# Attention by rows of 512 queries, with pieces of the projections and of the output between the units

## What is computed

```
xn = ln(x, g_norm)
q = (xn @ Wq).reshape(b, n, HEADS, DIM_HEAD).transpose(0, 2, 1, 3)
k, v = split(xn @ Wkv)                      # one head of 64 each
k, v = concat([null_k, k]), concat([null_v, v])
q, k = l2norm(q) * q_scale, l2norm(k) * k_scale
sim = einsum('bhid,bjd->bhij', q, k) * 8 + rel_pos_bias        # causal
out = einsum('bhij,bjd->bhid', softmax(sim), v)
z = ln(merge_heads(out) @ Wout, g_out)
s = 127 / max(abs(z), axis=-1)
return x + (clip(round(z * s), -128, 127) / s) @ ternary.T * weight_scale + bias
```

## Time and profile before

| | us |
|---|---|
| median of 3 runs | 1786.13 (1785.21 to 1788.83) |
| the profiled execution | 1786.81 |
| its span, first to last instruction | 1784.5 |
| PE busy | 1604.5 |
| DVE busy | 1407.2 |
| ACT busy | 1141.8 |
| POOL busy | 1421.9 |

### The profile page before, as it was taken

One profiled execution on the slowest core, in us unless ns is written; L12 is line 12 of the kernel. 1 busy time (PEld: TensorE's weight loads), 2 busy tenths in 40 slices (PEclk: granted clock), 3 DMA queues, 4 the chain that ended last, 5 costly groups with the idle time before them and its releaser, 6 DMA issues.

```text
span 1784.5 us, 46777 instructions
## 1 busy us (share of the span) xinstructions
PE 1604.5 (90%) x15122; PEld 1079.6 (60%) x15122; DVE 1407.2 (79%) x2569; ACT 1141.8 (64%) x2195; POOL 1421.9 (80%) x934
## 2 busy tenths in 40 slices
PE   3786897899999999998995898799999999998997
PEld 1443554577777777776552455477777777776553
DVE  4885898788888888884765798688888888887576
ACT  1342555587787788777441555477887887787441
POOL 3564666799999999997673566799999999999574
PEclk9998999899999999998997999899999999999998
DMA  6000012011112111100023002021111111110023
GB/s 186 1 0 21 25 29 59 13 37 35 28 37 49 25 37 37 29 21 14 30 71 102 25 29 65 1 47 26 38 37 25 37 37 41 26 32 13 7 71 100
DMA packets 41302, 68.84 MB, mean 39 GB/s; under 512 B 8880, under 2 KB 9392, under 8 KB 41136
## 3 DMA queue, kind: packets, MB, share of 16 engines
q1 hardware_dynamic: 36512, 58.12, 13.3%
q10 hardware_dynamic: 4640, 8.54, 1.4%
HBM read 58.11 MB, written 8.54 MB: 37 GB/s over the span
## 4 chain that ended last, share of the span: by engine, by line
PE 44%; issue 26%; POOL 17%; DVE 9%; ACT 1%; DVEq 1%; POOLq 1%; DMA 1%; SPq 0%; ACTq 0%
PE ps L1162 21%; PE ps L1135 10%; PE ps L1138 10%; DVE work L930 5%; POOL rinv L491 4%; POOL work L496 4%; POOL work L523 3%; POOL qo L454 2%; POOL work L541 2%; PE ps L1204 1%; DVE work L958 1%; POOL rstd L486 1%; DVE denom L955 1%; POOL work L498 1%; POOL work L462 1%
## 5 line engine op out<-in xcount | busy, mean ns | idle before, releaser
L511 POOL TENSOR_TENSOR work<-work 128x1024 f16<-128x1024 f32 (+2 forms) x576 | 978.2, 1733 | 44.2 <-ACT work L644 41.6
L930 DVE SCALAR_TENSOR_TENSOR work<-ps,tab 128x1024 f32<-128x1024 f32 (+3 forms) x640 | 668.7, 1059 | 141.3 <-PE ps L1138 139.4
L644 ACT ACTIVATE work<-work 128x1024 f32<-128x1024 f32 (+3 forms) x640 | 578.2, 924 | 207.3 <-DVE work L930 203.4
L1162 PEld LDWEIGHTS ps<-vals,work 128*128 128x128 bf16 (+1 forms) x8704 | 545.3, 98 | 115.8 <-POOL work L511 2.2
L1162 PE MATMUL ps<-vals,work 128*128 128x129 f16 x8704 | 600.5, 221 | 1.9 <-POOL work L511 1.8
L1135 PE MATMUL ps<-qo,kT 128*128 128x512 f16 (+3 forms) x1280 | 344.2, 351 | 20.8 <-DVE work L930 15.0
L1138 PE MATMUL ps<-qo,kT 128*128 128x512 f16 (+3 forms) x1280 | 342.1, 349 | 0.0
L1106 PE MATMUL ps<-wq,work 128*128 128x512 f16 x768 | 178.0, 390 | 20.4 <-DVE work L863 20.4
L1138 PEld LDWEIGHTS ps<-qo,kT 128*128 128x128 f16 x1280 | 123.2, 98 | 117.5 <-issue 3.3
L1204 PE MATMUL ps<-wout,work 128*128 128x512 f16 x768 | 175.0, 385 | 0.0
L1106 PEld LDWEIGHTS ps<-wq,work 128*128 128x128 f16 x768 | 74.6, 100 | 113.5 <-issue 34.2
(11 more groups left out here) (131 smaller groups left out, 1727.0 us busy)
## 6 DMA issues: line engine op xcount, KB each, us to landing
tab<-bias_table SPq DMA_DIRECT2D x64, 512.0 KB, 4.7
work<-in_x SPq DMA_DIRECT2D x32, 256.0 KB, 2.6
tab<-in_x SPq DMA_DIRECT2D x32, 256.0 KB, 2.7
out_x<-work ACTq DMA_DIRECT2D x32, 256.0 KB, 2.2
work<-in_L_cond_Wq SPq DMA_DIRECT2D x1, 2048.0 KB, 12.8
work<-in_L_cond_Wout SPq DMA_DIRECT2D x2, 1024.0 KB, 10.3
qo<-in_L_cond_w SPq DMA_DIRECT2D x1, 1024.0 KB, 9.5
qo<-in_L_cond_b SPq DMA_DIRECT2D x2, 256.0 KB, 4.2
```

The costliest lines, as they stand in the source:

```text
L511: pool.tensor_tensor(low[:, k % LRING, :, c0:512], probs[:, r, :, c0:512], high[:, r, :, c0:512], ALU.subtract).then_inc(low_pool, 1)
L644: act.activation(probs[:, k % RING, :, c0:512], probs[:, k % RING, :, c0:512], ACT.Exp).then_inc(expd, 1)
L930: dve.scalar_tensor_tensor(out=probs[:, k % RING, :, c0:512], in0=ps[:, 2 * (k % 2):2 * (k % 2) + 2, c0:512], scalar=SCORE, in1=tab[:, :, ...
L1162: last = pe.matmul(ps[:, sum_bank(i, q), (t % SUMS) * VS:(t % SUMS + 1) * VS], parts[:, rings[part], e, s * P:(s + 1) * P], vals[:, j, :], ...
```

## The change

The loop over batches is gone, and the program is written out. The attention is one sequence of 640 units over eight rows of 512 queries (four of each batch), row by row: in a row the eight head pairs, in a head pair the units. Row 0 and row 4 (i = 0) have 32 units, rows 1 and 5 64, rows 2 and 6 96, rows 3 and 7 128. Before the first unit only the first 8 of the 32 projection tiles are done, as before, with a bank of its own for each step. The steps of the other 24 tiles, and of the first 28 of 32 output tiles, are given to slots, one slot for each unit. Two tables (`B_FROM`, `C_FROM`) say near which slot a tile starts, `B_STAGES` and `C_STAGES` in which order its steps come and with which gaps, and `spread` fills the slots: on PE at most one piece a slot, between `score` and `weigh`; on VectorE and ScalarE behind the slot's bias or exponential (ACT1: ahead of the exponential). All these pieces use one PSUM bank (7), and a piece waits until the one before it has been read out of the bank. Their working tiles are single. The last four output tiles follow the attention with banks of their own.

Also changed: the rings of `probs` and `low` have 8 and 6 places in place of 10 and 8, weighing follows 5 units behind; VectorE takes two low halves of a head pair in a row with i = 3, one with i = 2, none else; the transposed output is split into halves behind the transposition (out of PSUM, on ScalarE and VectorE); z is copied out of PSUM first, the gain is applied on VectorE, 1 / standard deviation goes into the scale of the quantisation; the bias table is loaded in pieces by a list. 308 pieces on PE wait for bank 7.

```diff
-TW = S
-NEARER = (0, 1, 5, 9)
...
+KS = 22
+ROWS = B * NB
+UNITS = [(r, hp, j) for r in range(ROWS) for hp in range(HP) for j in range(4 * (r % NB) + 4)]
 NU = len(UNITS)
-RING = 10
-LRING = 8
-WORK = 16912
-LAG = 6
+NUMBER = {u: n for n, u in enumerate(UNITS)}
+ROW_START = [NUMBER[r, 0, 0] for r in range(ROWS)] + [NU]
+RING = 8
+LRING = 6
+LAG = 5
...
+DVE_LOW = {3: (5, 11), 2: (5,), 1: (), 0: ()}
...
+WEIGH, DRAINS, NULLS, STORES = ({} for _ in range(4))
+for _n, (_r, _hp, _j) in enumerate(UNITS):
+    for _q in range(3):
+        WEIGH.setdefault(_n + LAG + late(_q, _j), []).append((_n, _q))
+for _r in range(ROWS):
+    for _hp in range(HP):
+        _end = NUMBER[_r, _hp, 4 * (_r % NB) + 3]
+        for _q in range(3):
+            DRAINS.setdefault(_end - 2 + _q + LAG + 1, []).append((_r, _hp, _q))
+        NULLS[_end - 2] = (_r, _hp)
+        STORES[_end + LAG + 2] = (_r, _hp)
+LAST_SLOT = NU + LAG + 3
+AHEAD = 8
+B_FROM = {8: 0, 9: 16, 10: 32, 11: 48, 12: 80, 13: 102, 14: 124, 15: 146, 16: 186, 17: 208, 18: 230, 19: 252,
...
+C_FROM = {0: 42, 1: 56, 2: 70, 3: 84, 4: 108, 5: 130, 6: 152, 7: 174, 8: 204, 9: 220, 10: 240, 11: 262,
...
+B_STAGES = (("load_x", "SP", 0), ("stat", "DVE", 3), ("power", "POOL", 1), ("norm", "DVE", 2),
+            ("X", "PE", 1), ("x_high", "ACT1", 0), ("x_low", "DVE", 0),
+            ("P0a", "PE", 1), ("P0b", "PE", 1), ("q0", "ACT", 0), ("P1a", "PE", 1), ("P1b", "PE", 1), ("q1", "ACT", 0),
+            ("P2", "PE", 1), ("q2", "ACT", 0), ("square", "ACT", 0), ("sum", "DVE", 1), ("length", "POOL", 1),
+            ("unit", "DVE", 3), ("high", "ACT", 1), ("low", "POOL", 1), ("KV", "PE", 2), ("kv", "DVE", 0),
+            ("T0", "PE", 1), ("t0", "ACT1", 0), ("T1", "PE", 1), ("t1", "DVE", 0))
+C_STAGES = (("reload_x", "SP", 0), ("O0", "PE", 0), ("o_high0", "ACT1", 0), ("o_low0", "DVE", 0),
+            ("O1", "PE", 1), ("o_high1", "ACT1", 0), ("o_low1", "DVE", 0),
+            ("Za", "PE", 1), ("Zb", "PE", 1), ("Zc", "PE", 1), ("z_copy", "ACT", 0),
+            ("z_stat", "DVE", 1), ("z_power", "POOL", 1), ("z_gain", "DVE", 0), ("residual", "POOL", 1),
+            ("quant_a", "DVE", 1), ("quant_b", "DVE", 1), ("Y", "PE", 1), ("y_copy", "ACT1", 0),
+            ("F", "PE", 1), ("final", "DVE", 0), ("store", "SP", 1))
+AFTER = {"X": "P2", "P0a": "unit", "square": "low", "sum": "KV", "high": "T1", "load_x": "X",
+         "O0": "Zc", "z_copy": "quant_b", "quant_b": "Y", "y_copy": "F", "reload_x": "store"}
...
+def spread():
+    slots = {e: {} for e in ("SP", "DVE", "POOL", "PE", "ACT1", "ACT")}
+    last, placed = {}, {}
+    jobs = sorted([(s + 12, 0, g, s) for g, s in B_FROM.items()] + [(s, 1, g, s) for g, s in C_FROM.items()])
+    for _, kind, g, at in jobs:
+        for stage, engine, gap in (B_STAGES, C_STAGES)[kind]:
+            at = max(at + gap, last.get((kind, stage), -1) + 1, last.get((kind, AFTER.get(stage)), -1) + 1)
+            if stage == "KV" and KS <= g < KS + NT:
+                at = max(at, ROW_START[NB] + LAG + 3)
+            if stage == "T0" and g >= 12:
+                at = max(at, placed["O1", g - 12] + 1)
+            if engine == "PE":
+                chunk = "abc".index(stage[-1]) if stage[-1] in "abc" else 0
+                more = {"P0a": 2, "P1a": 2, "Za": 3}.get(stage, 1)
+                while not chunk and any(at + k in slots["PE"] for k in range(more)):
+                    at += 1
+                if chunk == 0:
+                    for k in range(more):
+                        slots["PE"][at + k] = []
+                slots["PE"][at] = [(stage, g)]
+                assert kind or at + 2 < ROW_START[g // 4], (stage, g, at)
+            else:
+                slots[engine].setdefault(at, []).append((stage, g))
+            last[kind, stage] = placed[stage, g] = at
+    return slots
...
+        def bank(kind, g):
+            if kind in "XP0P1P2KVT0T1" and g < AHEAD:
+                return ("X", "P0", "P1", "P2", "T0", "T1", "KV").index(kind)
+            if kind in "O0O1ZYF" and g >= B * NT - 4:
+                return {"O0": 0, "O1": 1, "Z": 2 + g % 2, "Y": 4, "F": 5 + g % 2}[kind]
+            return 7
...
+            def square(g):
+                h = before_b(g)
+                act.wait_ge(b_qc, 3 * g + 3)
+                if h >= 0:
+                    act.wait_ge(b_hi, 2 * h + 2)
+                    act.wait_ge(b_lo, 2 * h + 2)
+                act.activation(qn[ub(g)], q_sb[ub(g)][:, 0:QKW], ACT.Square).then_inc(b_sq, 1)
...
+            for s in range(LAST_SLOT):
+                for stage, g in SIDE["ACT1"].get(s, ()):
+                    side[stage](g)
+                if s < NU:
+                    exps(s)
+                if s in NULLS:
+                    null_part(*NULLS[s])
+                if s in STORES:
+                    store_o(*STORES[s])
+                for stage, g in SIDE["ACT"].get(s, ()):
+                    side[stage](g)
...
+            def unit_length(g):
+                u, w = g % 2, ub(g)
+                dve.wait_ge(b_rinv, g + 1)
+                dve.tensor_tensor(qn[w].rearrange("p (h d) -> p h d", d=DH),
+                                  q_sb[w][:, 0:QKW].rearrange("p (h d) -> p h d", d=DH),
+                                  rinv[:, u, :].unsqueeze(2).to_broadcast([P, H + 1, DH]), ALU.mult
+                                  ).then_inc(b_qn, 1)
+                if g >= 1:
+                    dve.wait_ge(b_snd, g)
+                dve.tensor_tensor(sn_part[:, :], q_sb[w][:, QKW:V0], rinv[:, u, 0:H], ALU.mult).then_inc(b_snp, 1)
+                dve.wait_ge(b_qn, g + 1)
+                dve.tensor_tensor(kn[w], qn[w][:, H * DH:QKW], qk_scale[:, :], ALU.mult).then_inc(b_kn, 1)
+                dve.wait_ge(b_snp, g + 1)
+                if g >= 2:
+                    dve.wait_ge(b_pn, g - 1)
+                dve.scalar_tensor_tensor(out=sn[:, u, :], in0=sn_part[:, :], scalar=SCORE,
+                                         in1=null_shift[:, :], op0=ALU.mult, op1=ALU.add).then_inc(b_snd, 1)
...
+            def z_gain(g):
+                dve.scalar_tensor_tensor(out=y[uc(g)], in0=y[uc(g)], scalar=zmv[:, g % 2, 0:1], in1=gout_b[:, :],
+                                         op0=ALU.subtract, op1=ALU.mult).then_inc(c_t, 1)
+                dve.wait_ge(c_t, g + 1)
+                if g >= 1:
+                    dve.wait_ge(c_amx, g)
+                dve.tensor_reduce(amax[:, :], y[uc(g)], AX.X, ALU.max, apply_absolute_value=True).then_inc(c_am, 1)
...
+            def quant_b(g):
+                h = before_c(g)
+                dve.wait_ge(c_y1, g + 1)
+                dve.tensor_scalar(y[uc(g)], y[uc(g)], -128.0, ROUND, ALU.max, ALU.add).then_inc(c_y2, 1)
+                dve.wait_ge(c_y2, g + 1)
+                if h >= 0:
+                    dve.wait_ge(c_yT, h + 1)
+                dve.tensor_scalar(yq[uc(g)], y[uc(g)], ROUND, None, ALU.subtract).then_inc(c_yq, 1)
...
-                skewed(dve, NT, [(c_stat, 3), (c_final, 7), (c_quant, 4), (c_norm, 3)])
...
+            for s in range(LAST_SLOT):
+                for due in DRAINS.get(s, ()):
+                    drain(*due)
+                if s < NU:
+                    bias(s)
+                for stage, g in SIDE["DVE"].get(s, ()):
+                    side[stage](g)
+                if s - 2 in LOW_ORDER[True]:
+                    low_part(s - 2)
...
-                skewed(pe, NT, [(b_project, 3), (b_turn_x, 2), (b_turn_q, 5)])
...
-                for hp in range(HP):
-                    for k in range(NU):
-                        score(hp, k)
-                        weigh_slot(hp, k)
-                for k in range(NU, NU + LAG + 1):
-                    weigh_slot(HP - 1, k)
...
+            before = None
+            for s in range(LAST_SLOT):
+                if s < NU:
+                    score(s)
+                for stage, g in SIDE["PE"].get(s, ()):
+                    if before and stage[-1] not in "bc":
+                        pe.wait_ge(*out_of(*before))
+                    side[stage](g)
+                    before = stage.rstrip("abc"), g
+                for n, q in sorted(WEIGH.get(s, ())):
+                    weigh(n, q)
+            pe.wait_ge(*out_of(*before))
+            last = B * NT - 4
+            for s in range(4 + 3):
```

More of the change, by code:

```diff
@@ L413, in _ @@
+            store(B * NT - 1)
+            for u in range(2):
+                sp.wait_ge(c_out[u], 16 * (B * NT // 2))
         @block.gpsimd
         def _(pool):
[L415 removed]
+            for s, n in ((M[0]["g"], 1), (M[1]["g"], 1)):
                 pool.sem_inc(s, n)
@@ new lines, in residual @@
+            def residual(g):
+                pool.wait_ge(c_xr[g % 2], 16 * (g // 2 + 1))
+                pool.tensor_tensor(xb[uc(g)], xb[uc(g)], fbias_b[:, :], ALU.add).then_inc(c_xb, 1)
+            for s in range(AHEAD + 4):
+                for stage, lag in ((low_halves, 4), (length, 3), (power, 0)):
+                    if 0 <= s - lag < AHEAD:
```

(21 more changed lines are left out.)

1183 lines of the change are left out of this document (588 added, 595 removed).

## The result

The changed kernel takes 2072.9 us (median of 4 runs, 2069.6 to 2076.8), the kernel before 1785.7 beside it: a ratio of 1.161 (95% interval 1.158 to 1.164), slower. The forecast was 1899, range 1795 to 2060. The direction is right, the size is not; what came is rival (c), at its 2070.

What follows compares the result with a forecast made beforehand. VectorE with lock waits (1420 us) was to pass PE (1355) in the merged stage. Head 251.4, merged stage 1591 (1442 by rows, times 1.10, plus 5), tail 53.8 and 2.3 outside gave 1899 us, range 1795 to 2060.

Steps and rivals of the forecast that it cites:

- rival (c): Merged stage: chains of waits stretch the dense rows (1, 2, 3, 5, 6) by 1.35; end 2070, 1990 and more; chance 0.15.
- Head, tail, PE's own work: First score at 251.4 us, tail of 53.8 us, PE's bare work in the merged stage 1355 us.
- The sum without waits: Whole kernel summed for PE, if no piece makes anybody wait: 1718.5 us.
- Rows 0 and 4 at 60 to 80 us: Sign in the merged stage: the two rows of only diagonal units take 60 to 80 us each.
- Locks: Merged stage: 280 VectorE operations wait 0.75 us each for the SBUF port shared with GpSimd, 210 us.
- row maxima of 1442: Merged stage: the busiest engine's time in each of the eight rows, 1442 us together.
- In-order losses: Merged stage: imperfect overlap of engines in fixed order, with bank 7 in common; 10% on 1442, giving 1586 us.
- Walking the sixteen units: Under (c), sixteen units from 240 followed through their durations: 40 us without locks, 48 with, for 34.6 of PE work.
- The clock: Sign that the forecast is wrong: granted clock of the merged stage clearly below 0.99; in no term.
- gaps on PE without a releaser: Sign that the forecast is wrong: "issue" gaps on PE from the program being written out instead of looped; in no term.
- (a): Merged stage: pieces fit in, every bank 7 wait and lock falls into slack; 1718 to 1780 us; chance 0.13.
- (b): Merged stage: locks cost little, only in-order losses remain, 10% on PE's rows; 1812, 1790 to 1840 us; chance 0.20.

Runs made afterwards that it cites:

- e13: e1 plus TensorE's part of every piece in its slot, on fixed operands, with no waits for or by pieces: 1712.7 us.
- e1: The changed kernel with the attention by rows alone, without the 24 projection and 28 output tiles between the units: 1430.8 us.
- e5: e1 with VectorE writing the sums straight into the place of the results, where ScalarE scales them: 1374.0 us.
- e3: The changed kernel with GpSimd's low-half subtractions replaced by powers of about the same time on few columns: 1970.3 us.
- e14: The changed kernel with all waits kept, TensorE's projections between the units cut to their first and last matrices: 1959.8 us.
- e4: The changed kernel with the weighing ahead of the piece in each slot on PE: 1993.9 us.
- e7: The changed kernel with one more slot before Y and between O0 and O1 in the planner's table: 2058.1 us.
- e6: e5 with the sizes of the kernel before: 10 scores, 8 low halves, weighing 6 units behind: 1335.4 us.
- e10: The changed kernel with six of VectorE's operations for the pieces cut to 16 of 512 columns between the units: 2043.6 us.

## Why the prediction was wrong in size

- **Head, tail, PE's own work: right.** 247.8, 45.6 and 1384 us at full rate. The sum without waits, 1718.5, was met by e13 to 6 us, though by two errors: the attention alone is dearer than I had it (e1, 106 us), and bare pieces fill part of that.
- **Rows 0 and 4 at 60 to 80 us: too low.** They took 84.3 and 93.9 from first bias to first bias. I costed ScalarE's sixteen activations there, but overlooked that the drain waits for the eight of the store; e5, which takes this wait away, has these rows at 44.3 and 46.7.
- **Locks, 280 x 0.75 = 210 us on VectorE: the mechanism right, the size too high.** 0.32 each. In my order of causes they were what lifts VectorE over PE, to 1420; in fact VectorE is busy 1296 us (my 1210 and the 90 that e3 shows), in no stage full, and the row maxima of 1442, mostly VectorE's, are not what bounds. That removing the locks gives 102 us (e3) is their part in the chain of waits. GpSimd's full subtraction, which I had expected above 2.02 us, did not lengthen: 1935 ns now, 2021 in the earlier trace rows.
- **In-order losses, 10% of 1442: this step failed.** It came from the projections, where 8.86 us pass for 8.2. There one stream of tiles has a bank for each of its pieces. Here two streams share bank 7 and stand in one order with scores and weighing, on four engines. The stage took 1774 us, 23% over my 1442; and on PE, with no assumption on VectorE, 25% over e13's 1417, what PE needs in the same slots. No row is spared: 84, 189, 266, 382, 94, 194, 281 and 284 us where I had 56, 144, 224, 307, 70, 162, 242 and 236. Walking the sixteen units had given 40 us for 34.6 without locks and 48 with them. That walk of rival (c) was the better evidence; it had a chance of 0.15.
- **The clock: in no term.** I had named it as what would prove me wrong, at clearly below 0.99. It is 0.94 in the merged stage, 92 us of PE's busy time. It is not independent: in the table it moves with the waits. The other sign named there, gaps on PE without a releaser, stayed small: 12 us in the merged stage.
- **Rivals.** (a) is what e13 shows for PE without waits for the pieces; the changed kernel is 293 us above the end of its range. (b) had the engine right, not VectorE but PE's slots, and the 10% wrong. (c) has the size, and by e13 and e14 the mechanism: waits handed on through all engines. That its total came to within 11 us of the merged stage is partly luck: its dense rows took 1312 us for 1363, rows 0 and 4 178 for 150, row 7 284 for 250.
- **Slips in the sums.** 16 x 60.6 + 388 is 1358, not 1355; the eight rows add up to 1441; and by 280 waits on top of 1210 VectorE falls level with PE at 0.5 us, not 0.4. None moves the forecast by more than 3 us.

Of the 354 us between the forecast's sum without waits, 1718.5, and 2072.9, the parts measured alone are the lock (102), the piece ahead of the weighing (79) and the sums' wait and small rings (95, in the attention alone). They overlap: e4 and e5 with e7 bring 90 and not the sum of the three. The rest was not taken apart further. That all pieces share one bank was not tried alone. The waits of PE that the view shows in the merged stage come to 293 us: 76 end with a bias (scores), 70 with an operand made elsewhere (Y's and X's), and some 135 with an instruction that reads bank 7, which for 28 of them also makes the piece's own operand. How much of the 135 a second bank would give back stays open; it would have to come from scores or sums.

## What to carry to other kernels

When idle time of one stage is to be filled with pieces of another in a fixed order on every engine, add not only the busy times but follow one piece through all engines: it waits in each queue behind the other stream, and while an engine waits for a late piece, the ready work behind it waits too. Put the ready work first (79 us here), and count what is given up to make room, buffers above all (95 us here, in the attention alone). A cheap way to know beforehand is to run the pieces of the busiest engine on fixed operands in their places: here it told 1713 us for that engine alone, and most of the 360 us between that and the full kernel is waiting (251 more of idling on PE) and the lower clock that goes with it (79 us).

## What the runs showed of the hardware

I had not expected how closely TensorE's clock goes with its waits. The time at 1.2 GHz was 2 us for 48 of idling (e6), 52 for 116 (e1), 140 for 230 (e3), 218 for 298 (the change), 320 for 412 (e14). The sum of idling is not all: e5 idles 75 us, its scores waiting 1.1 us at most at a time, and has 3 us at the lower level; e13 idles only 47 us, with waits for a bias of up to 4.1 us, and has 31. Where there are long waits, a removed one pays more than its length: e5 took 41 us from PE's idle time and 57 from e1's run. In the timeline above the lower level follows upon a single wait of 2.22 us.

Two things on the lock. Its wait does not shrink with the operation: 16 columns of the gain take 0.81 us in e10, where a maximum of 16 columns takes 0.17, which leaves about 0.6 of waiting; at 512 columns the gain takes 1.36 us in the changed kernel and 1.07 in e3. And in e3 GpSimd's powers have two SBUF inputs and last 1.82 us, nearly as long as the subtractions that they replace, yet the multiplication keeps its 1.28 us, also in the 19 of 24 cases in which it starts while a power is running:

```profile
L633 POOL TENSOR_TENSOR pw_out<-pw_in,minus_half 128x9 f32<-128x9 f32 x400 | 724.7, 1821 | 316.2 <-ACT arena L758 225.7 <-PE ps L1333 88.9
```

The Trainium skill's page SBUF — State Buffer, section Who interferes with whom, gives the port pair to the first instruction for its whole length. The subtractions here agree with that; the long power on nine columns does not, and the measurement decides: a GpSimd instruction's length alone does not tell what VectorE will wait.
